# Maxima turned in mid-iteration and an expert program without a loop, in a one-core convolution, attention and expert kernel

## The chip, the core and the metric

The kernel runs on one core of a Trainium2 chip. A core has TensorE (PE, matrix products and transposes into PSUM banks), VectorE (DVE), ScalarE (ACT), GpSimd (POOL) and SyncE (SP, which here only issues DMA transfers). Each engine works through its own program in order; they meet at semaphores. The metric is the device time of the whole program in microseconds, the median of the runs.

## What is computed

The input is x, 16 images of 128 channels and 32 x 32 pixels. A convolution attention block is added to it, then, with pixels as tokens of 128 channels, a causal attention block, then a mixture of eight experts of which each token uses two. All of it is in float32.

```python
x = x + _L0_conv_ref(_gn(x), ...)      # 8 heads of queries, keys and values from a strided depthwise convolution
t = _to_tokens(x)
t = t + _L1_attn_ref(_ln_t(t), L1_attn_WQ, L1_attn_WK, L1_attn_WV)
t = t + _L1_ffn_ref(_ln_t(t), L1_ffn_router_w, L1_ffn_w1, L1_ffn_w2, L1_ffn_w3)

# in _L0_conv_ref
attn = jnp.einsum('bnqd,bdl->bnql', q, k) / HEAD_DIM ** 0.5
attn = jax.nn.softmax(attn, axis=-1)
ctx = jnp.einsum('bnql,bld->bnqd', attn, v)

# in _L1_ffn_ref: gates holds the weights of the two best experts of a token, 0 for the others
h = jax.nn.silu(h1) * h3
y = jnp.einsum('neh,ech->nec', h, w2)
out = jnp.einsum('ne,nec->nc', gates, y)
```

## The kernel before

Three stages run one after the other, each a block with its own program for each engine.

**Convolution attention** (conv_attention). Each image has 32 rows of queries; four rows are a pair's work (PAIR_ROWS), so an image is a period of PAIRS = 8 iterations. For a softmax without overflow each score needs its row's maximum. PE computes the scores of a row into one of two s_bank banks (L600), DVE reduces them to negated maxima (row_max, L395), four times per pair. PE then turns the pair's maxima into rows (turn_maxes, L608, m_bank), ACT copies the high part (max_high, L482), DVE the low part (max_low, L401), and SP puts both under the queries by two small transfers (shift_rows). PE later computes the scores again, transposed and with the maxima already subtracted (shifted_scores, L618), ACT takes exponentials (exps, L489), PE sums the values (values, L630, o_bank), ACT copies the context, PE turns it (turn_context, L638), DVE divides by the sums (normalise, L413 and L415). All this is spread over iterations: in iteration i PE scores pair i + 3 (LEAD = 3), turns the maxima of pair i + 2, computes the shifted scores of pair i, sums pair i - 1 and turns the context of pair i - 2. Iterations 0, 2, 4 and 6 also have a chunk of queries (L565), 1 the convolution (L543), 3 and 7 an output projection (L586), 7 a group mean (group_means, L526), which needs DVE's statistics (L346). The order on each engine is written out by hand in its `period`.

**Attention and routing** (attention_and_routing) is not touched. It writes every token twice, once per chosen expert, into a table in HBM sorted by expert, and a list of 2 x 136 = 272 tiles of 128 rows with the expert of each.

**Expert tiles** (expert_tiles). Each tile n passes through: SP loads its rows (L1443) into one of RING = 8 buffers, when the scatter of tile n - 8 has landed (y_sent); PE turns them (turn_rows, L1549, x_bank); ACT and DVE split them into a high and a low part (L1480, L1516); PE multiplies with w1 and w3 of the tile's expert (up, L1563 and L1566, six products of 342 columns); ACT takes silu (L1494), DVE multiplies by it and by the gate (L1531); PE turns the hidden rows (turn_hidden, L1574, three transposes), ACT copies them (L1485); PE multiplies with w2 (down, L1582, six passes), DVE copies y (L1522), POOL adds it to the output rows by an indirect transfer (L1457). PE's order for tile n is: expert number of n, rows of n + 1, up n, hidden of n - 1, down n - 2.

The helper over_tiles writes this as 34 turns of eight tiles: two turns straight, 15 in a loop, 16 in a second loop, one straight. In the loops tile numbers and semaphore values are registers. The expert number is read from the list in SBUF into a register by expert_of (L1554); down takes the number that up read, except in tiles 0 and 1 of a turn, which read it again:

```python
down(n - 2, i % 2, experts[i - 2] if i >= 2 else expert_of(n - 2))
```

## Time and profile before

| | us |
|---|---|
| median of 3 runs | 2365.29 (2364.75 to 2367.83) |
| profiled execution | 2363.08 |
| its span, first to last instruction | 2361.3 |
| convolution attention, to about | 860 |
| attention and routing, about | 880 to 1700 |
| expert tiles, first turned rows to last product | 1711 to 2352 |

The profile is one execution. "Busy" is the time in which an engine had an instruction; matmuls overlap and their ends are modelled, so a small idle time of PE is larger in truth. PEld is the loading of PE's stationary operand, PEq and PEldq are PE's sequencer, SPq is SP's queue. A bracket in the order of time gives the idle time of the engine just before an instruction and whose work ended it; "issue" means that the profile shows nothing it waited for. The granted clock is the share of 2.4 GHz that PE had.

### The profile page before, as it was taken

How to read it: one execution, taken by the hardware profiler on the slowest of the kernel's cores; microseconds unless marked ns; L12 is line 12 of the kernel's file. 1: busy time of each engine (PE TensorE's matmuls, PEld its weight loads, DVE VectorE, ACT ScalarE, POOL GpSimd, SP SyncE). 2: the span in 40 equal slices, each digit the busy share in tenths (PEclk: the TensorE clock that was granted, in tenths of full speed). 3: DMA queues.
4: the chain of work that ended last, by engine and by line, in shares of the span. 5: the costliest groups of instructions: out<-in, count | busy, mean ns of one | idle time of the engine just before them, and what ended most of it. 6: DMA issues, size and time to landing. Idle time of an engine off the chain costs nothing. (4 is left out here: it accounts for less than half of the span.)

```text
span 2361.3 us, 46450 instructions
## 1 busy us (share of the span) xinstructions
PE 2031.8 (86%) x11636; PEld 1462.9 (62%) x11637; DVE 1444.6 (61%) x4059; ACT 997.0 (42%) x2116; POOL 1006.0 (43%) x1345
## 2 busy tenths in 40 slices
PE   5999999999999974988888878886099999999998
PEld 4555555555555532655555555554098888888887
DVE  4666666666666642787677777876444444444443
ACT  1455554545555531433333333332044444444443
POOL 2121221212122111145544544555467777777776
PEclk7999999999999996999999999998599999999999
DMA  5222222222222212011111111111134444444443
GB/s 198 61 68 59 69 60 63 66 58 68 57 68 62 63 66 86 19 38 59 46 41 57 44 45 45 53 38 47 55 51 57 56 56 57 57 58 57 56 56 47
DMA packets 175904, 139.58 MB, mean 59 GB/s; under 512 B 33694, under 2 KB 163142, under 8 KB 175558
## 3 DMA queue, kind: packets, MB, share of 16 engines
q0 software_dynamic: 55808, 52.50, 13.9%
q1 hardware_dynamic: 120005, 86.09, 13.1%
q8 instruction: 31, 0.51, 0.1%
q14 instruction: 60, 0.48, 0.1%
HBM read 31.47 MB, written 46.71 MB: 33 GB/s over the span
## 5 line engine op out<-in xcount | busy, mean ns | idle before, releaser
L1457 POOL DMA_INDIRECT out<-f_y,f_rows x272 | 424.1, 1559 | 45.4 <-POOL f_waited L1455 39.8
L395 DVE TENSOR_REDUCE neg_max<-s_bank 128x2 f32<-128x512 f32 x512 | 329.9, 686 | 172.0 <-PE s_bank L600 171.5
L1531 DVE SCALAR_TENSOR_TENSOR f_hidden<-f_silu,f_rows,f_h_bank 128x341 f32<-128x341 f32 x272 | 155.2, 571 | 259.7 <-ACT f_silu L1494 206.9
L489 ACT ACTIVATE probsT<-st_bank 128x512 f32<-128x512 f32 x512 | 277.4, 593 | 36.6 <-PE st_bank L618 35.4
L975 POOL DMA_INDIRECT routed<-a_rows,a_target_idx x256 | 252.2, 985 | 74.5 <-issue 74.5
L1305 PE MATMUL a_score_bank<-a_eT,a_gT 128*128 128x512 f32 x512 | 253.2, 619 | 19.6 <-DVE a_causal_probs L1043 11.0
L630 PE MATMUL o_bank<-probsT,v_ones 128*64 128x512 f32 x1024 | 249.4, 608 | 0.0
L287 POOL TENSOR_TENSOR waited<-nothing 128x1 int32<-128x1 int32 x64 | 12.1, 190 | 547.5 <-DVE q_low L384 547.4
L1582 PE MATMUL f_y_bank<-w,f_hiddenT 114*128 (+1 forms) x1632 | 233.1, 278 | 0.9 <-DVE f_y L1522 0.6
L1494 ACT ACTIVATE f_silu<-f_h_bank 128x341 f32<-128x341 f32 x272 | 124.2, 457 | 211.1 <-PE f_h_bank L1566 164.3
L1582 PEld LDWEIGHTS f_y_bank<-w,f_hiddenT 114*128 114x128 f32 (+1 forms) x1632 | 203.2, 191 | 12.2 <-issue 11.4
L600 PEld LDWEIGHTS s_bank<-k_stack,q_stack 96*128 96x128 f32 x1024 | 141.7, 194 | 108.4 <-issue 106.4
L1563 PE MATMUL f_h_bank<-f_w_high,f_xT_high 128*128 x544 | 199.5, 369 | 0.0
L600 PE MATMUL s_bank<-k_stack,q_stack 96*128 96x256 f32 x1024 | 191.5, 310 | 6.0 <-DMA q_stack<-q_high 5.2
L962 POOL TENSOR_TENSOR a_causal_probs<-a_causal_probs,a_tril 128x128 f32<-128x128 f32 x128 | 58.2, 455 | 305.5 <-ACT a_causal_probs L1217 304.5
L1217 ACT ACTIVATE a_causal_probs<-a_score_bank,a_row_neg_max 128x128 f32<-128x128 f32 (+7 forms) x128 | 94.7, 740 | 220.1 <-DVE a_row_neg_max L1035 204.6
L618 PE MATMUL st_bank<-q_stack,k_stack 98*128 98x512 f32 x512 | 184.2, 439 | 0.1
L1563 PE MATMUL f_h_bank<-f_w_low,f_xT_high 128*128 x544 | 173.0, 320 | 0.0
L1035 DVE TENSOR_REDUCE a_row_neg_max<-a_score_bank 128x1 f32<-128x1024 f32 x128 | 156.7, 1224 | 22.7 <-PE a_score_bank L1305 22.0
L1322 PE MATMUL a_sum_bank<-a_val,a_causal_probsT 128*128 128x128 f32 x1152 | 153.9, 280 | 2.6 <-issue 2.3
L1322 PEld LDWEIGHTS a_sum_bank<-a_val,a_causal_probsT 128*128 128x128 f32 x1152 | 143.1, 195 | 10.5 <-issue 6.9
L1305 PEld LDWEIGHTS a_score_bank<-a_eT,a_gT 128*128 128x128 f32 x512 | 91.1, 198 | 90.1 <-issue 77.2
(197 smaller groups left out, 3647.6 us busy)
## 6 DMA issues: line engine op xcount, KB each, us to landing
q_stack<-q_high SPq DMA_DIRECT2D x512, 64.0 KB, 2.4
f_rows<-routed SPq DMA_DIRECT2D x272, 66.0 KB
q_stack<-q_low POOLq DMA_DIRECT2D x256, 64.0 KB, 2.6
a_staged<-X SPq DMA_DIRECT2D x16, 512.0 KB, 3.0
out<-X SPq DMA_DIRECT2D x16, 512.0 KB
X<-in_x SPq DMA_DIRECT2D x1, 6144.0 KB, 22.1
out<-f_y,f_rows POOLq DMA_INDIRECT x272
q_stack<-max_rows SPq DMA_DIRECT2D x256, 4.0 KB
```

Of the source, the lines that this page charges most:

```text
L395: dve.tensor_reduce(neg_max[:, i % 2, CT * j:CT * (j + 1)], s_bank[h % 2][:], AX_X, ALU.max, negate=True).then_inc(max_ready, 1)
L489: act.activation(probsT[:, i % 2, c, lt, :], st_bank[lt][:], ACT.Exp).then_inc(exp_done, 1)
L600: last = pe.matmul(s_bank[h % 2][:, t, :], q_stack[0:STACK, h, t * P:(t + 1) * P], k_stack[0:STACK, slot, :], start=(t == 0), stop=(t == C ...
L618: pe.matmul(st_bank[lt][:], k_stack[:, slot, lt * P:(lt + 1) * P], q_stack[:, h:h + 2, :].rearrange("p h c -> p (h c)"), start=True, stop= ...
L630: last = pe.matmul(o_bank[HALF * c:HALF * (c + 1), :], v_ones[:, slot, lt, :], probsT[:, i % 2, c, lt, :], start=(lt == 0), stop=(lt == LT ...
L975: pool.indirect_dma_start(out=routed, out_offset=bass.IndirectOffsetOnAxis(ap=target_idx[:, slot, t, k:k + 1], axis=0), in_=rows[:, slot, ...
L1035: dve.tensor_reduce(neg_max[:, i % 2:i % 2 + 1], s_bank[i % 2][:], AX_X, ALU.max, negate=True).then_inc(max_ready, 1)
L1305: last = pe.matmul(s_bank[i % 2][:, 512 * h:512 * (h + 1)], gT[:, slot, i * P:(i + 1) * P], eT[:, slot, 512 * h:512 * (h + 1)], start=True ...
L1322: last = pe.matmul(o_bank[:], probsT[:, i % 2, t, :], val[:, slot, t, :], start=(t == 0), stop=(t == i))
L1457: pool.indirect_dma_start(out=out, out_offset=bass.IndirectOffsetOnAxis(ap=rows[:, i, TOKEN:TOKEN + 1].bitcast(I32), axis=0), in_=y[:, i, ...
L1563: pe.matmul(bank[:, 0:PADDED], xT_high[:, i % 2, :], parts[part][:, of_expert], start=(part == 0), stop=False, skip_group_check=True)
L1582: last = pe.matmul(y_bank[:], hiddenT[0:m, slot, j, :], w2[0:m, bass.ds(e, 1), j, :], start=(j == 0), stop=(j == CHUNKS - 1))
```

## The change

It has three parts; nothing that is computed changes.

In the convolution attention PE turns the maxima of pair i + 2 not at the head of iteration i but between scores 1 and shifted scores 1. ACT copies them between its exponentials for the first and the second half of the pair, and DVE's max_low goes behind normalise.

In the expert tiles PE's program is written out for all 272 tiles. Tile numbers and semaphore values are constants, each expert number is read once, two tiles ahead (AHEAD = 2), and kept in a register until down. The rows are turned two tiles ahead, into two x_bank banks in turn, and split into four xT buffers. PE's order becomes: up n, expert number and rows of n + 2, down n - 2, hidden of n - 1. The waits on x_out before turning rows, on gated before up and on h_out before turning the hidden rows are gone. ACT does silu before the split of the next rows, DVE the gating before it. ACT, DVE, POOL and SP keep their loops.

The scatters add to the output rows in both kernels alike.

```diff
@@ conv_attention, DVE
                             row_max(scored[0], scored[2], 1)
+                        turned = pair(b, slot, i - 2)
+                        if has(turned[0]):
+                            normalise(*turned)
                         turning = pair(b, slot, i + LEAD - 1)
                         if has(turning[0]):
                             max_low(*turning)
-                        turned = pair(b, slot, i - 2)
-                        if has(turned[0]):
-                            normalise(*turned)
@@ conv_attention, ACT
                         turning = pair(b, slot, i + LEAD - 1)
+                        if has(b):
+                            exps(b, i, 0)
                         if has(turning[0]):
                             max_high(*turning)
                         if has(b):
-                            exps(b, i)
+                            exps(b, i, 1)
@@ conv_attention, PE
-                        if has(turning[0]):
-                            turn_maxes(*turning)
                         if has(b):
                             shifted_scores(b, slot, i, 0)
...
                         if has(scored[0]):
                             scores(*scored, 0)
                             scores(*scored, 1)
+                        if has(turning[0]):
+                            turn_maxes(*turning)
                         if has(b):
                             shifted_scores(b, slot, i, 1)
@@ expert_tiles, ACT
                     act.wait_ge(x_turned, n + 1)
-                    wait(act, h_full, n - 1)
-                    act.activation(xT_high[:, slot, :], x_bank[:], ACT.Copy).then_inc(x_high_done, 1)
+                    wait(act, h_full, n - 2 * AHEAD + 1)
+                    act.activation(xT_high[:, slot, :], x_bank[slot % 2][:], ACT.Copy).then_inc(x_high_done, 1)
...
-                    if not last_one(n):
-                        x_evacuate(n + 1, (i + 1) % 2)
                     act.wait_ge(h_full, n + 1)
                     wait(act, gated, n - 1)
                     act.activation(silu[:, i % 2, :], h1_bank[i % 2][:, 0:HIDDEN], ACT.Silu).then_inc(silu_done, 1)
+                    if not beyond(n + AHEAD):
+                        x_evacuate(n + AHEAD, (i + AHEAD) % (2 * AHEAD))
@@ expert_tiles, PE
-                def turn_rows(n, q, i):
-                    pe.wait_ge(row_in[i], 16 * (q + 1))
-                    wait(pe, x_out, n)
-                    pe.transpose(x_bank[:], rows[:, i, 0:P], ident[:]).then_inc(x_turned, 1)
...
+                def turn_rows(n):
+
+                    pe.wait_ge(row_in[n % RING], 16 * (n // RING + 1))
+                    pe.transpose(x_bank[n % 2][:], rows[:, n % RING, 0:P], ident[:]).then_inc(x_turned, 1)
...
-                def up(n, i, e):
+                    return pe.value_load(table[0:1, 1, n:n + 1], min_val=0, max_val=EXPERTS - 1)
+
+                def up(n, e):
+
                     pe.wait_ge(x_out, n + 1)
-                    wait(pe, gated, n - 1)
...
-                    wait(pe, h_out, n)
...
-                def body(n, q, i, k):
-                    if first(n):
-                        turn_rows(0, 0, 0)
-                    experts[i] = expert_of(n)
-                    if not last_one(n):
-                        turn_rows(n + 1, q + (i == RING - 1), (i + 1) % RING)
-                    up(n, i, experts[i])
-                    if not first(n):
-                        turn_hidden(n - 1, (i + 1) % 2)
-                    if not (isinstance(n, int) and n < 2):
-                        down(n - 2, i % 2, experts[i - 2] if i >= 2 else expert_of(n - 2))
-
-                over_tiles(pe, body)
...
+                for n in range(ALL):
+                    up(n, experts[n])
+                    if n + AHEAD < ALL:
+                        experts[n + AHEAD] = expert_of(n + AHEAD)
+                        turn_rows(n + AHEAD)
+                    if n >= 2:
+                        down(n - 2, experts.pop(n - 2))
+                    if n >= 1:
+                        turn_hidden(n - 1)
```

PE in the convolution attention, an iteration after a chunk of queries, before (the name behind "waits" is a semaphore, max_ready counts DVE's maxima):

```order
L608 MATMUL m_bank<-ident,neg_max 128x128 [waits m_low_done,max_ready]
L618 MATMUL st_bank<-q_stack,k_stack 128x512 [waits exp_done,m_in1]
L618 MATMUL st_bank<-q_stack,k_stack 128x512 [waits exp_done]
L638 MATMUL c_bank<-ident,ctxT 128x128 [waits ctx_done,ctxT_full]
L638 MATMUL c_bank<-ident,ctxT 128x128 x3
L600 MATMUL s_bank<-k_stack,q_stack 128x256 [waits max_ready,q_low_in3,q_in3]
L600 MATMUL s_bank<-k_stack,q_stack 128x256
L600 MATMUL s_bank<-k_stack,q_stack 128x256 [waits max_ready]
L600 MATMUL s_bank<-k_stack,q_stack 128x256
L618 MATMUL st_bank<-q_stack,k_stack 128x512 [waits exp_done] x2
```

and now:

```order
L620 MATMUL st_bank<-q_stack,k_stack 128x512 [waits exp_done,m_in1]
L620 MATMUL st_bank<-q_stack,k_stack 128x512 [waits exp_done]
L640 MATMUL c_bank<-ident,ctxT 128x128 [waits ctx_done,ctxT_full]
L640 MATMUL c_bank<-ident,ctxT 128x128 x3
L602 MATMUL s_bank<-k_stack,q_stack 128x256 [waits max_ready,q_low_in3,q_in3]
L602 MATMUL s_bank<-k_stack,q_stack 128x256
L602 MATMUL s_bank<-k_stack,q_stack 128x256 [waits max_ready]
L602 MATMUL s_bank<-k_stack,q_stack 128x256
L610 MATMUL m_bank<-ident,neg_max 128x128 [waits m_low_done,max_ready]
L620 MATMUL st_bank<-q_stack,k_stack 128x512 [waits exp_done] x2
```

The turn into m_bank stood first and now stands behind the four s_bank matmuls, so that the first wait on max_ready is that of s_bank.

DVE in the same iteration, before:

```order
L395 TENSOR_REDUCE neg_max<-s_bank 128x2 [waits m_full,s_full]
L395 TENSOR_REDUCE neg_max<-s_bank 128x2 [waits s_full]
L401 TENSOR_TENSOR max_rows<-m_bank,max_rows 8x128 [waits m_high_done]
L413 RECIPROCAL rsum<-c_bank 128x2x4 [waits c_full]
L415 TENSOR_TENSOR context<-c_bank,rsum 128x256 [waits rsum_ready]
L395 TENSOR_REDUCE neg_max<-s_bank 128x2 [waits s_full] x2
```

and now:

```order
L395 TENSOR_REDUCE neg_max<-s_bank 128x2 [waits m_full,s_full]
L395 TENSOR_REDUCE neg_max<-s_bank 128x2 [waits s_full]
L413 RECIPROCAL rsum<-c_bank 128x2x4 [waits c_full]
L415 TENSOR_TENSOR context<-c_bank,rsum 128x256 [waits rsum_ready]
L401 TENSOR_TENSOR max_rows<-m_bank,max_rows 8x128 [waits m_high_done]
L395 TENSOR_REDUCE neg_max<-s_bank 128x2 [waits s_full] x2
```

max_rows (max_low) went behind the two operations of normalise.

PE in the expert tiles, from the expert load before down in tile 0 of a looped turn to that of tile 1, before (TENSOR_LOAD with the two ISA behind it is one expert load; ISA and REGISTER_ALU run in PE's sequencer):

```order
L1554 TENSOR_LOAD table
L1554 ISA x2
L43 REGISTER_ALU [waits f_h_out]
L1582 ISA [waits f_y_out]
L1582 MATMUL f_y_bank<-w,f_hiddenT 128x128
L1582 ISA
L1582 MATMUL f_y_bank<-w,f_hiddenT 128x128
L1582 ISA
L1582 MATMUL f_y_bank<-w,f_hiddenT 128x128
L1554 ISA
L1554 TENSOR_LOAD table
L1554 ISA x2
```

and now, from the expert load of a tile to the head of the next up:

```order
L1557 TENSOR_LOAD table
L1557 ISA x2
L1554 MATMUL f_x_bank<-ident,f_rows 128x128 [waits f_row_in5]
L1585 ISA [waits f_y_out,f_h_out]
L1585 MATMUL f_y_bank<-w,f_hiddenT 128x128
L1585 ISA
L1585 MATMUL f_y_bank<-w,f_hiddenT 128x128
L1585 ISA
L1585 MATMUL f_y_bank<-w,f_hiddenT 128x128
L1576 MATMUL f_hT_bank<-ident,f_hidden 114x128 [waits f_gated]
L1576 MATMUL f_hT_bank<-ident,f_hidden 114x128 x2
L1566 ISA [waits f_x_out]
```

One load is left where two stood around down, the rows of a later tile are turned ahead of down, and the register operations that carried waits (REGISTER_ALU) are gone.

## Rows read from the trace of the kernel before

**Rows 1.** Busy time by stretch (PE, PEld, DVE, ACT, POOL), clock, DMA share, GB/s

```profile
37.00:860.00 823.00, 775.88 (x3852) 466.26 (x3853) 544.48 (x1158) 414.82 (x823) 150.03 (x325) 0.99 0.25 62
1713.00:2346.00 633.00, 616.65 (x4322) 565.67 (x4322) 301.31 (x811) 302.88 (x813) 467.41 (x536) 1.00 0.43 56
```

**Rows 2.** Waits in total, whole run: us, times, longest

```profile
PE m_bank L608 <- DVE neg_max L395: 40.4, 81, 1.1
```

**Rows 3.** Order of time, PE, first stage: start, us, operation, idle before

```profile
434.10 1.88 PE L586 MATMUL front<-context,owT 128*128 128x512 f32 x4
435.82 0.27 PE L608 MATMUL m_bank<-ident,neg_max 128*128 128x128 f32 x1
...
445.74 0.74 PE L600 MATMUL s_bank<-k_stack,q_stack 96*128 96x256 f32 x4
447.63 0.33 PE L608 MATMUL m_bank<-ident,neg_max 128*128 128x128 f32 x1 [1.15 <-DVE neg_max L395]
447.81 0.73 PE L618 MATMUL st_bank<-q_stack,k_stack 98*128 98x512 f32 x2
...
448.73 0.72 PE L600 MATMUL s_bank<-k_stack,q_stack 96*128 96x256 f32 x4
...
453.65 0.33 PE L608 MATMUL m_bank<-ident,neg_max 128*128 128x128 f32 x1 [0.28 <-DVE neg_max L395]
```

**Rows 4.** Order of time, PE, expert tiles in the loop

```profile
2001.78 0.27 PE L1549 MATMUL f_x_bank<-ident,f_rows 128*128 128x128 f32 x1
...
2010.61 0.33 PE L1549 MATMUL f_x_bank<-ident,f_rows 128*128 128x128 f32 x1 [0.15 <-issue]
...
2013.42 0.33 PE L1549 MATMUL f_x_bank<-ident,f_rows 128*128 128x128 f32 x1 [0.22 <-issue]
...
2020.59 0.27 PE L1549 MATMUL f_x_bank<-ident,f_rows 128*128 128x128 f32 x1
```

**Rows 5.** One line's instructions, whole run: duration min/median/max ns

```profile
L1554 PEldq TENSOR_LOAD <-table x340: 295/301/489, 1711.3 to 2349.1; - x170
```

**Rows 6.** Order of time, PE, expert tiles of the first turn

```profile
1725.53 0.27 PE L1549 MATMUL f_x_bank<-ident,f_rows 128*128 128x128 f32 x1
...
1727.60 0.28 PE L1549 MATMUL f_x_bank<-ident,f_rows 128*128 128x128 f32 x1
```

**Rows 7.** Order of time, DVE, first stage

```profile
446.28 1.29 DVE L395 TENSOR_REDUCE neg_max<-s_bank 128x2 f32<-128x512 f32 x2 [0.92 <-PE s_bank L600]
...
456.00 0.21 DVE L346 BATCH_NORM_AGGREGATE mv<-bn_st 128x2 f32<-128x12 f32 x1
```

**Rows 8.** Chain of work, 2013 to 2045 us: start, us, what

```profile
2018.81 0.63 PE f_h_bank L1563 x4
2019.44 0.32 PE f_h_bank L1566 x2
```

**Rows 9.** Groups of instructions by line, 1720 to 2340 us: mean ns, idle before

```profile
L1485 ACT ACTIVATE f_hiddenT<-f_hT_bank 114x384 f32<-114x384 f32 x265 | 128.6, 485 | 0.0
```

**Rows 10.** Order of time, POOL, at the end

```profile
2346.68 1.56 POOL L1457 DMA_INDIRECT out<-f_y,f_rows  x1 [0.15 <-POOL f_waited L1455]
...
2348.63 1.56 POOL L1457 DMA_INDIRECT out<-f_y,f_rows  x1 [0.16 <-POOL f_waited L1455]
```

**Rows 11.** Order of time, DVE and SP, two trips of the ring

```profile
2000.02 0.29 DVE L1522 COPY f_y<-f_y_bank 128x128 f32<-128x128 f32 x1
...
2004.17 0.29 DVE L1522 COPY f_y<-f_y_bank 128x128 f32<-128x128 f32 x1
...
2004.30 0.34 SPq L1443 DMA_DIRECT2D f_rows<-routed  x1
...
2008.76 0.33 SPq L1443 DMA_DIRECT2D f_rows<-routed  x1
```

**Rows 12.** The page, DMA queues (packets, MB, share), issues (KB each, us to landing)

```profile
q8 instruction: 31, 0.51, 0.1%
...
q_stack<-q_high SPq DMA_DIRECT2D x512, 64.0 KB, 2.4
```

More of the change, by code:

```diff
@@ L482, in max_high, with exps @@
                     act.activation(max_rows[:, i % 2, 0, :], m_bank[0:MAXES, :], ACT.Copy).then_inc(m_high_done, 1)
-                def exps(b, i):
-                    wait(act, o_full, pair_no(b, i) - 1)
-                    for c in range(CHUNKS_PER_PAIR):
-                        for lt in range(LT):
-                            act.wait_ge(st_full, PAIR_EXPS * pair_no(b, i) + LT * c + lt + 1)
-                            act.activation(probsT[:, i % 2, c, lt, :], st_bank[lt][:], ACT.Exp).then_inc(exp_done, 1)
+                def exps(b, i, c):
+                    if c == 0:
+                        wait(act, o_full, pair_no(b, i) - 1)
+                    for lt in range(LT):
+                        act.wait_ge(st_full, PAIR_EXPS * pair_no(b, i) + LT * c + lt + 1)
+                        act.activation(probsT[:, i % 2, c, lt, :], st_bank[lt][:], ACT.Exp).then_inc(exp_done, 1)
                 def evacuate_context(b, slot, i):
@@ L1348 @@
 PADDED = HIDDEN + 1
+AHEAD = 2
 def expert_tiles(nc, table, routed, out, ntok, ident, w1, w3, w2, weights_in):
@@ L1377, in expert_tiles @@
         y = sb("y", [P, RING, P])
-        x_bank = ps("x_bank", [P, P])
+        x_bank = [ps(f"x_bank{i}", [P, P]) for i in range(2)]
         h1_bank = [ps(f"h1_bank{i}", [P, 512]) for i in range(2)]
@@ L1423, in first, with beyond @@
             return isinstance(n, int) and n == 0
-        def last_one(n):
-            return isinstance(n, int) and n == ALL - 1
+        def beyond(n):
+            return isinstance(n, int) and n >= ALL
         def entry(n):
@@ L1488, in body @@
                     if first(n):
-                        x_evacuate(0, 0)
-                    if not last_one(n):
-                        x_evacuate(n + 1, (i + 1) % 2)
+                        for early in range(AHEAD):
+                            x_evacuate(early, early)
                     act.wait_ge(h_full, n + 1)
@@ L1525, in body @@
                     if first(n):
-                        x_low(0, 0)
-                    if not last_one(n):
-                        x_low(n + 1, (i + 1) % 2)
+                        for early in range(AHEAD):
+                            x_low(early, early)
                     dve.wait_ge(silu_done, n + 1)
@@ L1533, in body @@
                                              op0=ALU.mult, op1=ALU.mult).then_inc(gated, 1)
+                    if not beyond(n + AHEAD):
+                        x_low(n + AHEAD, (i + AHEAD) % (2 * AHEAD))
                     if not (isinstance(n, int) and n < 2):
@@ L1561, in up @@
                     for bank, parts in outs:
                         for part in range(2):
-                            pe.matmul(bank[:, 0:PADDED], xT_high[:, i % 2, :], parts[part][:, of_expert],
+                            pe.matmul(bank[:, 0:PADDED], xT_high[:, n % (2 * AHEAD), :], parts[part][:, of_expert],
                                       start=(part == 0), stop=False, skip_group_check=True)
                     for bank, parts in outs:
-                        last = pe.matmul(bank[:, 0:PADDED], xT_low[:, i % 2, :], parts[0][:, of_expert],
+                        last = pe.matmul(bank[:, 0:PADDED], xT_low[:, n % (2 * AHEAD), :], parts[0][:, of_expert],
@@ L1567, in up, with turn_hidden @@
                                          start=False, stop=True, skip_group_check=True)
                     last.then_inc(h_full, 1)
-                def turn_hidden(n, slot):
+                def turn_hidden(n):
                     pe.wait_ge(gated, n + 1)
-                    wait(pe, h_out, n)
                     for j in range(CHUNKS):
-                        last = pe.transpose(hT_bank[:, j, :], hidden[:, slot, j * CHUNK:(j + 1) * CHUNK], ident[:])
+                        last = pe.transpose(hT_bank[:, j, :], hidden[:, n % 2, j * CHUNK:(j + 1) * CHUNK], ident[:])
@@ L1575, in turn_hidden, with down @@
                     last.then_inc(h_turned, 1)
-                def down(n, slot, e):
+                def down(n, e):
                     pe.wait_ge(h_out, n + 1)
@@ L1581, in down @@
                         m = min(CHUNK, HIDDEN - j * CHUNK)
-                        last = pe.matmul(y_bank[:], hiddenT[0:m, slot, j, :], w2[0:m, bass.ds(e, 1), j, :],
+                        last = pe.matmul(y_bank[:], hiddenT[0:m, n % 2, j, :], w2[0:m, bass.ds(e, 1), j, :],
                                          start=(j == 0), stop=(j == CHUNKS - 1))
                     last.then_inc(y_full, 1)
-                def body(n, q, i, k):
-                    if first(n):
-                        turn_rows(0, 0, 0)
-                    experts[i] = expert_of(n)
-                    if not last_one(n):
-                        turn_rows(n + 1, q + (i == RING - 1), (i + 1) % RING)
-                    up(n, i, experts[i])
-                    if not first(n):
-                        turn_hidden(n - 1, (i + 1) % 2)
-                    if not (isinstance(n, int) and n < 2):
-                        down(n - 2, i % 2, experts[i - 2] if i >= 2 else expert_of(n - 2))
-                over_tiles(pe, body)
-                turn_hidden(ALL - 1, 1)
-                down(ALL - 2, 0, expert_of(ALL - 2))
-                down(ALL - 1, 1, expert_of(ALL - 1))
+                experts = {n: expert_of(n) for n in range(AHEAD)}
+                for n in range(AHEAD):
+                    turn_rows(n)
+                for n in range(ALL):
[7 more added lines that the diff above has]
+                        turn_hidden(n - 1)
+                down(ALL - 2, experts.pop(ALL - 2))
+                turn_hidden(ALL - 1)
+                down(ALL - 1, experts.pop(ALL - 1))
 def build(nc, dram, out):
```

10 lines of the change are left out of this document (4 added, 6 removed).

## The prediction

> **What bounds the kernel now.** I read the page first, for where PE is busy, then the busy time of each stretch, then each stage's order of time on TensorE (PE). The program has three stages that do not overlap: the convolution attention (37 to 860 us), attention with routing (880 to 1700 us) and the expert tiles (1711 to 2352 us). In the first and the third PE is busy 94% and 97% of the time, at a granted clock of 0.99 and 1.00, its upper level of 2.4 GHz [rows 1]; VectorE (DVE), ScalarE (ACT) and GpSimd (POOL) all stand well below that. The change touches these two stages alone. Attention with routing, 820 us, keeps its program, and I cost it at nothing.
>
> In the first stage the order of time shows where PE is not fed. An iteration is one pair: shifted scores 0, turned context, scores 0 and 1, shifted scores 1, values, scores 2 and 3, and sometimes queries or a projection. It begins with the turn of the maxima (m_bank, L608), and that turn waits for the fourth row maximum of the pair scored just before: 40.4 us in 81 waits [rows 2]. After queries the idle time shown is 0.28 us, after a projection none, and in the one iteration of eight that has neither 1.15 us [rows 3]. A shown idle time begins at the modelled end of the matmul before, and where nothing waits the next one starts 0.16 us before that end (434.10 + 1.88 against 435.82). So a wait really costs 0.16 us more than is shown: 40.4 + 81 x 0.16 = **53 us**.
>
> In the third stage the wait table holds nearly nothing for PE, yet tiles differ. From one x_bank transpose to the next, tiles of the loop take from 2.05 to 2.81 us (2010.61 to 2013.42 is one of two that take 2.81); eight take 18.81 [rows 4]. The slow ones begin with an idle time that ends on "issue": no engine was late, PE's own sequencer was. Tiles 0 and 1 of a turn load two expert numbers where the others load one: 340 loads for 272 tiles [rows 5]. The first turn of eight is written without a loop in this kernel already, and there a tile takes 2.07 us [rows 6], its neighbours 2.05 and 2.06. That is the pace of PE itself on this work.
>
> **Part 1, the maxima turned later.** The m_bank turn goes behind scores 1. What is late next is scores 0, which needs the third row maximum of the pair before (its bank), and scores 1, which needs the fourth. In the iteration without extra work scores 3 end near 446.32 and the fourth maximum at 446.28 + 1.29 = 447.57 [rows 3, 7]. Shifted scores 0 and the context take 447.81 to 448.73 = 0.92 us, scores 0 0.24 more, so scores 1 would come at 447.48, 0.1 to 0.15 us too early. Once in each of 16 images: 2.4 us stay. After queries their matmuls come on top and nothing stays.
>
> A second wait takes back a part. In iteration 7 the group mean (L526) waits for DVE's statistics, which end at 456.00 + 0.21 whenever PE comes; PE now comes 0.44 us earlier (0.28 + 0.16) and waits it out [rows 3, 7]. With 14 such iterations: 6 us back. ACT's copy of the maxima now stands between the exponentials of shifted scores 0 and 1. It lasts 0.27 us; ACT is busy 415 of 823 us [rows 1] and idle 0.3 us just there, before the second pair of exponentials, so I take nothing, and 0.1 us in each of 128 iterations, 13 us, as the bad bound. DVE copies the low part after normalising, 0.6 us later, and SP's two small transfers follow it; their result is needed only two iterations, some 12 us, later. On SP they keep their place behind the queries' transfers. Nothing is queued that could not wait. Sum of stage one: 53 - 2 - 6 = **45 us**, between 28 and 53.
>
> **Part 2, TensorE's expert program.** It removes 68 expert loads, the register arithmetic for tile numbers and wait values, the loop, and the waits on buffers that other waits imply. Each tile is left with one load. The price of the doubled load is in the rows: a slow tile 2.81 against 2.06. If every tile ran at 2.06, a turn would take 16.5 instead of 18.8. The Trainium skill ("DMA: Bandwidth & Descriptors", Latency and other measured facts) gives a tensor load a floor of about 600 ns; the row's instruction is 0.30 us long, and the whole slow tile 0.75 longer. By the page alone the 68 loads would be an estimated 41 us.
>
> Two blocking waits stay in PE's stream: x_out before up, h_out with y_out before down. With the new order (up, turn of rows n+2, down n-2, turn of hidden n-1) I time them: up is 0.63 + 0.32 = 0.95 us [rows 8], x 0.11, down 0.67 and hidden 0.33, sum 2.06. From the start of hidden's turn to h_out: 0.49 for the three transposes, 0.05 to ACT, 0.48 for ACT's copy [rows 9] = 1.02, and 0.16 until PE can use it (the gap from DVE's maximum to PE's matmul is 0.06, 447.57 to 447.63 [rows 3, 7]; the rest is the sequencer's own step). The following up and x hide 0.33 + 0.95 + 0.11 = 1.39. Slack 0.2 us. For y: DVE does hidden, x_low and then y in a row after silu, and y ends 2.63 us into a tile, again 0.3 before the next down. POOL needs 1.95 us for a scatter back to back [rows 10], just under 2.06. So no engine but PE bounds the tile.
>
> **The ring of eight row buffers** is nearer. A row load for tile n+8 goes out only when the scatter of tile n has landed. From DVE's y copy to that load pass 4.28 us (2000.02 to 2004.30) and 4.59 us (2004.17 to 2008.76) [rows 11]; the load's landing is not shown, the nearest row is a 64 KB transfer on the same queue, 2.4 us [rows 12]. Trip: 6.7 to 7.0 us. Now rows are turned one tile earlier (two tiles ahead, though at the end of up), and y is copied as late as 2.34 us into its tile: with a tile of T us the ring has 3T + 0.95 - 0.29 = 3T + 0.66, that is 6.84 at T = 2.06. The trips need T = 2.01 to 2.11. PE takes tiles in order, so the later trips set the pace: I take **2.11 us**, 16.9 us a turn. 31 turns stand in the loops: 31 x (18.8 - 16.9) = 59; the turns at both ends bring 1 more. Stage three: **60 us**, between 37 (T = 2.20) and 77 (T = 2.05: 31 x 2.4 + 3).
>
> The tail after the last matmul is POOL's scatters and stays. The profiled execution took 2363.1 us, 2361.3 of it span; 2363.1 - 45 - 60 = 2258. The median of the runs lies 2.2 us above the profiled one, so **2260 us**.
>
> **The rivals.**
> Forecast, around 2260 (2240 to 2278): 0.52.
> *The ring binds harder*: scatters and loads come closer together and a trip takes 7.3 us or more; T = 2.20 or above, stage three gives 37 or less, the time is 2283 to 2300. For it: two trips read close together already differ by 0.3 us, and one part in ten more is enough. Against it: the DMA engines are busy 43% of the time only [rows 1]. The fast first turn says nothing here, since its rows were loaded ahead. 0.20. The Trainium skill ("DMA: Bandwidth & Descriptors", Queues, rings and completion order) says that a DMA engine goes round its queues packet by packet; the straight program adds code packets to those engines, which no run here shows next to the ring. It is counted in this rival.
> *The first stage's wait only moves*: to scores 0 or to the exponentials, leaving 10 us of 45; 2295. Against it: PE has 0.92 us of other work ahead of scores 0. 0.10.
> *Neither binds*: T = 2.05 and all 53 us: 2235. 0.10.
> *Slower*: code. A straight program has to be fetched; a loop is not. The run had 31 packets, 0.51 MB, of code on queue 8 [rows 12]. If PE's sequencer sat out a fetch as long as a 64 KB load, 2.4 us, every four tiles, that is 68 x 2.4 = 163 us against the 105 gained: 2423. It decides from 3.1 us a turn (105 over 34). Against it: the straight first turn ran at PE's own pace [rows 6]. 0.04. The Trainium skill ("Runtime: NRT & Kernel Launch", Instruction fetch mechanics) calls such crossings mostly hidden; the straight turn agrees.
> *It does nothing*: the slow tiles are slow for another reason than the second load, and the maxima's gain is lost: within 0.2%. 0.02. Between the cases lie the other 0.02.
>
> **How the numbers follow.** The range runs from the floor of 2235 to 2300, where the ring at T = 2.20 meets a small loss in stage one. It holds the forecast's case (0.52), about 0.14 of the ring's, 0.08 of the moved wait's and 0.09 of the floor's, 0.83 in all. A measurement of this kernel can tell about 0.2%, 5 us, from no change. Only the last two rivals are not clearly faster, and a little is left for a mixture of losses: faster 0.94, same 0.02, slower 0.04.
>
> **What would show it.** In stage one the m_bank wait vanishes from PE's table, a wait of some 0.1 us on scores 1 appears once an image, and L526 waits about 0.4 us longer. The stage ends near 815 us instead of 860. In stage three eight tiles take 16.4 to 17 us, all alike; 272 loads. If x_bank waits for a DMA, the ring has become the bound and T tells by how much; if PE idles on "issue", the sequencer still is; if on DVE or ACT, my slacks of 0.2 and 0.3 us were wrong. I would be wrong altogether if tiles without a loop ran no faster than 2.3 us.

## The result and the profile after

| | before | after |
|---|---|---|
| median, us | 2365.02 (2363.98 to 2367.83) | 2262.70 (2261.8 to 2264.08) |
| ratio, 95% interval | 1 | 0.9566 (0.955 to 0.9583) |
| profiled execution, its span | 2363.08, 2361.3 | 2261.92, 2260.1 |
| first to last turn of the maxima | 815.2 | 770.8 |
| first turned rows to last product of down | 639.7 | 582.9 |
| behind the last product | 10.3 | 10.0 |

The kernel became 102.3 us faster; 2260 had been forecast, 105 less. Busy time by stretch of the kernel after (the columns are those of [rows 1]):

```profile
37.00:818.00 781.00, 767.33 (x3868) 476.24 (x3870) 539.77 (x1161) 402.91 (x828) 155.12 (x325) 0.99 0.26 65
1668.00:2241.00 573.00, 564.20 (x4294) 550.23 (x4295) 262.71 (x807) 302.40 (x808) 464.83 (x533) 1.00 0.47 63
```

PE is now busy 98% of both stretches (before 94 and 97%) at the same granted clock. The two durations of the table come from the first and last start of three lines. First the kernel before, then after (duration min/median/max in ns, first and last start in us):

```profile
L608 PE MATMUL m_bank<-ident,neg_max x128: 269/328/476, 36.7 to 851.9; 128*128 128x128 f32 x128
L1549 PE MATMUL f_x_bank<-ident,f_rows x272: 274/275/449, 1711.3 to 2343.7; 128*128 128x128 f32 x136
L1582 PE MATMUL f_y_bank<-w,f_hiddenT x1632: 273/275/373, 1718.6 to 2351.0; 114*128 x182
```

```profile
L610 PE MATMUL m_bank<-ident,neg_max x128: 272/273/415, 38.0 to 808.8; 128*128 128x128 f32 x128
L1554 PE MATMUL f_x_bank<-ident,f_rows x272: 270/272/467, 1667.2 to 2241.5; 128*128 128x128 f32 x136
L1585 PE MATMUL f_y_bank<-w,f_hiddenT x1632: 272/275/373, 1674.2 to 2250.1; 114*128 x182
L1557 PEldq TENSOR_LOAD <-table x272: 295/301/490, 1665.6 to 2239.9; - x136
```

815.2 - 770.8 = 44.4 us went out of the first stage, 639.7 - 582.9 = 56.8 out of the third. The loads are 272, one for each tile.

**First stage.** All that PE waits for between 37 and 818 us (us in total, times, longest):

```profile
PE front L528 <- DVE mv L346: 12.6, 15, 2.3
PE st_bank L620 <- DMA q_stack<-max_rows: 0.5, 1, 0.5
PE m_bank L610 <- DVE neg_max L395: 0.2, 1, 0.2
PE s_bank L602 <- DVE neg_max L395: 0.2, 1, 0.2
```

Of the 40.4 us of [rows 2], 0.2 are left. The group mean (L528) waits 12.6 us; before it waited 7.0:

```profile
PE front L526 <- DVE mv L346: 7.0, 15, 1.9
```

The small stall at scores 1 is in no wait table, since the modelled ends of the matmuls cover it; it stands in the order of time, in the iteration that has no extra work:

```profile
425.97 0.99 PE L602 MATMUL s_bank<-k_stack,q_stack 96*128 96x256 f32 x4
426.80 0.27 PE L610 MATMUL m_bank<-ident,neg_max 128*128 128x128 f32 x1
...
431.60 0.72 PE L602 MATMUL s_bank<-k_stack,q_stack 96*128 96x256 f32 x4
432.16 0.28 PE L610 MATMUL m_bank<-ident,neg_max 128*128 128x128 f32 x1
...
433.82 0.38 PE L528 MATMUL front<-mv,group_mean 128*128 128x1 f32 x2 [0.73 <-DVE mv L346]
```

From scores 0 to the turn it is 0.83 us (425.97 to 426.80), in the next iteration 0.56: scores 1 wait 0.27 us, once an image. In this iteration DVE works through the maxima without a gap:

```profile
425.11 2.67 DVE L395 TENSOR_REDUCE neg_max<-s_bank 128x2 f32<-128x512 f32 x4 [1.16 <-PE s_bank L602]
```

**Third stage.** PE's wait table for 1668 to 2252 us, whole:

```profile
PE f_x_bank L1554 <- DMA f_rows<-routed: 6.8, 11, 1.4
PE f_y_bank L1585 <- ACT f_hiddenT L1488: 1.3, 2, 0.7
PE f_x_bank L1554 <- issue: 1.1, 1, 1.1
PE f_h_bank L1566 <- DVE f_xT_low L1520: 0.6, 1, 0.6
```

From one row turn to the next a tile takes 2.056 us in the median and (2241.5 - 1667.2) / 271 = 2.119 in the mean. What lifts the mean are single tiles. In the order of time:

```profile
2204.71 0.27 PE L1554 MATMUL f_x_bank<-ident,f_rows 128*128 128x128 f32 x1
2207.81 0.33 PE L1554 MATMUL f_x_bank<-ident,f_rows 128*128 128x128 f32 x1 [0.88 <-DMA f_rows<-routed]
2210.05 0.27 PE L1554 MATMUL f_x_bank<-ident,f_rows 128*128 128x128 f32 x1
```

Rows came late (3.10 us for the tile), and the tile behind it took 2.24 instead of 2.056. Such late turns, most of them shorter and many under the threshold of the wait table, make up the rest: 66 of the 271 turn-to-turn times are over 2.1 us.

The page has more code than [rows 12], 1.13 MB for 0.51, and no wait of PE goes with it. The DMA queues by stretch show where it is fetched: 7 packets of code in the whole stage before (1713 to 2346 us), 45 after (1668 to 2241 us), and one of them within the late tile above (2204.71 to 2207.81 us). The page first, then the three stretches:

```profile
q8 instruction: 69, 1.13, 0.2%
q8 instruction: 7, 0.11, 0.1%
q8 instruction: 45, 0.74, 0.5%
q8 instruction: 1, 0.02, 1.9%
```

The packets come every 12.6 us, once in six tiles, and the late turns keep their company. From 1712 us on, 117 of 248 turns start within 6 us of the start of a packet. Of the 60 that came over 2.1 us after the turn before, 52 are among these 117, and so are 15.3 of the 16.7 us that the tiles take above 2.056. In the five executions of this expert program together it is 62.0 of 79.5 us, in under half of the tiles. So the code does not hold up PE, but most of the long trips of the rows fall together with its packets. No run changed the packets alone; that they lengthen the trips is an inference from this timing.

### The profile page after: what moved, and what is told of

Same layout as the page of the kernel before. It is cut to its first block and busy times, and to the rows that moved or that the text cites. A ratio compares the mean times of both kernels' runs of the same rounds, so it can differ in the third digit from the quotient of the medians.

```text
span 2260.1 us, 45057 instructions
## 1 busy us (share of the span) xinstructions
PE 1970.1 (87%) x11636; PEld 1459.5 (65%) x11636; DVE 1401.3 (62%) x4059; ACT 983.6 (44%) x2116; POOL 1011.6 (45%) x1345
## 3 DMA queue, kind: packets, MB, share of 16 engines
q8 instruction: 69, 1.13, 0.2%
## 5 line engine op out<-in xcount | busy, mean ns | idle before, releaser
L620 PE MATMUL st_bank<-q_stack,k_stack 98*128 98x512 f32 x512 | 213.5, 484 | 0.6 <-DMA q_stack<-max_rows 0.5
L602 PE MATMUL s_bank<-k_stack,q_stack 96*128 96x256 f32 x1024 | 196.2, 312 | 6.7 <-DMA q_stack<-q_high 6.0
L1488 ACT ACTIVATE f_hiddenT<-f_hT_bank 114x384 f32<-114x384 f32 x272 | 133.7, 492 | 144.4 <-issue 82.9
```

What stands on the lines that cost most here:

```text
L602: last = pe.matmul(s_bank[h % 2][:, t, :], q_stack[0:STACK, h, t * P:(t + 1) * P], k_stack[0:STACK, slot, :], start=(t == 0), stop=(t == C ...
L620: pe.matmul(st_bank[lt][:], k_stack[:, slot, lt * P:(lt + 1) * P], q_stack[:, h:h + 2, :].rearrange("p h c -> p (h c)"), start=True, stop= ...
```

## The experiments

The stages of all kernels are compared by their traces, first to last start as above (us): turns of the maxima, and rows to last product. The ratio is that of the whole time to the kernel before on the same chip.

| kernel | maxima | expert tiles | ratio (95%) |
|---|---|---|---|
| before | 815.2 | 639.7 | 1 |
| after | 770.8 | 582.9 | 0.9566 (0.9550 to 0.9583) |
| only_maxima | 771.2 | 639.5 | 0.9774 (0.9747 to 0.9802) |
| only_experts | 815.5 | 578.1 | 0.9756 (0.9729 to 0.9784) |
| one_load | 815.2 | 591.7 | 0.9783 (0.9756 to 0.9810) |
| ring12 | 771.2 | 563.7 | 0.9470 (0.9443 to 0.9498) |
| stats_early | 756.8 | 580.1 | 0.9494 (0.9463 to 0.9525) |
| rows_first | 771.2 | 662.2 | 0.9895 (0.9870 to 0.9921) |
| twice_loaded | 771.4 | 599.8 | 0.9645 (0.9614 to 0.9676) |
| both12 | 756.8 | 563.9 | 0.9426 (0.9406 to 0.9446) |
| copied_twice | 770.5 | 579.7 | 0.9566 (0.9539 to 0.9592) |
| turn_only | 921.6 | 582.3 | 1.0197 (1.0170 to 1.0224) |
| no_loads | 770.7 | 587.6 | 0.9553 (0.9523 to 0.9583) |
| rows_first_no_loads | 770.5 | 649.7 | 0.9799 (0.9746 to 0.9852) |

The first stage repeats within 1 us. The third repeats within 5: five executions of one and the same expert program (after, only_experts, stats_early, copied_twice, turn_only) took 582.9, 578.1, 580.1, 579.7 and 582.3. Attention and routing between them (last projection to first row turn), which no kernel here changes, took from 802 to 840 us (839.9 in the kernel after, 813.3 in ring12). That is why whole times are not read to a few us here, and stages are.

### Each part alone

only_maxima is the first hunk of the change (all of conv_attention) without the others, only_experts the rest without the first.

> The kernel before with the changes in the convolution attention alone. My terms: the m_bank wait of 53 us goes, 2.4 us come back at scores 1 (0.16 once in each of 16 images) and 5.6 at the group mean (its wait 7.0 before, 12.6 after): 2365 - 45 = 2320 us, and the expert tiles as before, 639.8 us from the first turned rows to the last product. Rival: the two parts of the change are not independent (the second stage or the code fetch reacts), then the time is more than 5 us away from 2320.

> The kernel before with the changed expert tiles alone. The third stage took 582.9 us after against 639.8 before, 57 less: 2365 - 57 = 2308 us. The two parts alone then sum to 102, the whole change measured 102.3. Rival: they overlap or help each other, and the sum is off by more than 5 us.

The changed stage's line of only_maxima, then of only_experts:

```profile
L610 PE MATMUL m_bank<-ident,neg_max x128: 272/273/416, 37.5 to 808.7; 128*128 128x128 f32 x128
```

```profile
L1552 PE MATMUL f_x_bank<-ident,f_rows x272: 270/272/469, 1680.4 to 2250.1; 128*128 128x128 f32 x136
```

Each stage behaves as in the whole change and as if the other were not there: 44.0 us and 61.6. The whole times fell by 50.8 and 57.1 us on a chip on which the kernel before took 2332.9; the sum is 108, where 102 was expected. That is over the 5 us named as the sign of parts that depend on each other, and so is the first by itself (50.8 for 45). But the intervals of the ratios run from 46 to 59 us and from 50 to 63, so the whole times cannot decide it, and by the stages the excess of the first is not in its stage.

### What a second expert load costs

```diff
-                        down(n - 2, i % 2, experts[i - 2] if i >= 2 else expert_of(n - 2))
+                        down(n - 2, i % 2, experts[max(i - 2, 0)])
```

> The kernel before, with its loops, waits and register arithmetic, but tiles 0 and 1 of a turn take an expert number that is in a register already (of another tile, so their last product uses another expert's weights): the second load is left out, nothing else. If the doubled load was the whole price of the slow tiles, eight tiles fall from 18.8 to about 16.7 us (the looped tile's other six take 2.05 to 2.1), 31 x 2.1 = 65 us: 2300 us, no slower than the written-out program of the change in this stage. If the loop and its register arithmetic carried half of it, 2330. If the loads cost only their 0.30 us each, 62 x 0.30 = 19: 2346.

The stage fell by 48.0 us to 591.7. PE has 274 expert loads here for 340 before, 66 less (not 68: tiles 0 and 1 of the first turn have no down), so a load cost 0.73 us. That is most of what the whole expert program brings, and less than the 65 expected. The loop is left with two slow tiles at its head (order of time of one_load):

```profile
2002.16 0.27 PE L1549 MATMUL f_x_bank<-ident,f_rows 128*128 128x128 f32 x1
2004.66 0.32 PE L1549 MATMUL f_x_bank<-ident,f_rows 128*128 128x128 f32 x1 [0.18 <-issue]
2006.92 0.27 PE L1549 MATMUL f_x_bank<-ident,f_rows 128*128 128x128 f32 x1
2008.98 0.27 PE L1549 MATMUL f_x_bank<-ident,f_rows 128*128 128x128 f32 x1
```

2.50 and 2.26 us, then 2.06. PE still sits idle on "issue" at the head of a turn, with one load for each tile. Over the whole stage the medians of the eight tiles are 2.47, 2.27, 2.06, 2.05, 2.05, 2.19, 2.07 and 2.07: five of eight tiles run at PE's own pace with the old order of PE, its single x_bank and its extra waits, so most of what is left comes with the head of the loop's turn. Whether it is the branch or the register arithmetic was not separated, and why the sixth tile takes 2.19 neither. Together it is 28 us (591.7 to ring12's 563.7, below); the written-out program removes them too, but hands back 14 to 19 us to late rows.

The opposite test puts the second load back into the written-out program:

```diff
-                        down(n - 2, experts.pop(n - 2))
+                        e = experts.pop(n - 2)
+                        down(n - 2, expert_of(n - 2) if n % 8 < 2 else e)
```

> The changed kernel, still without a loop, with the expert number read a second time before down in tiles 0 and 1 of every eight, as before the change (68 loads more). If the load itself is what a slow tile cost, the 0.75 us come back in most of them: 68 x 0.6 to 0.75 = 41 to 51 us, a stage of 624 to 634. If the loop made the second load dear and PE's sequencer otherwise runs far enough ahead to hide it, the stage stays at 583.

599.8 us: 17 more than after, 0.26 for each of 66 loads (338 for 272). Neither case came true. In the order of time of twice_loaded:

```profile
2002.05 0.27 PE L1554 MATMUL f_x_bank<-ident,f_rows 128*128 128x128 f32 x1
2004.32 0.27 PE L1554 MATMUL f_x_bank<-ident,f_rows 128*128 128x128 f32 x1
2006.66 0.27 PE L1554 MATMUL f_x_bank<-ident,f_rows 128*128 128x128 f32 x1
```

And in its waits:

```profile
PE f_y_bank L1585 <- issue: 7.0, 22, 0.6
```

2.27 and 2.34 instead of 2.056. This turn is one of the better ones: over the stage the two tiles have a median of 2.41, and together they take 0.72 us a turn more than in the kernel after, while the other six take 0.22 less, with 8 waits for rows in the table instead of 11. So a load costs 0.36 us in its tile, and 0.26 in the stage. The same load costs 0.73 us in the loop: it has no price of its own. I read it as what PE's sequencer then needs above PE's own 2.056 us, a sequencer that in the loop needs the whole tile, with its register arithmetic, and without has some 0.37 us (0.73 - 0.36) to spare. Its total was not measured by itself.

The Trainium skill ("DMA: Bandwidth & Descriptors", Latency and other measured facts) has a tensor load at about 600 ns at least. Here the two differ: the instruction is 0.30 us long in the row of L1557 above, and what it took from a tile was 0.36 us in one program and 0.73 in the other.

### What holds the tile above 2.056

ring12 is the kernel after with twelve row and y buffers; the turns are of twelve tiles, the middle and the last one partly straight.

```diff
-RING = 8
+RING = 12
```

> The changed kernel with twelve row and y buffers instead of eight. A row load then has four tiles, 8 us, more before its rows are turned. If late rows are what lifts the mean tile from its median of 2.056 to 2.119 us, the wait of x_bank on the row load vanishes, every tile takes 2.05 to 2.06, the mid-way drain of the scatters is hidden too, and the stage loses 271 x 0.063 = 17 us: 2246 us. If only the waits shown for x_bank (6.8 us) go, and the tile of 2.24 us behind each of them has a cause of its own, 2256. If the ring isn't it, 2263.

```profile
L1555 PE MATMUL f_x_bank<-ident,f_rows x272: 270/272/472, 1640.7 to 2196.0; 128*128 128x128 f32 x136
L1586 PE MATMUL f_y_bank<-w,f_hiddenT x1632: 272/275/372, 1647.8 to 2204.4; 114*128 x182
```

563.7 us, 19 less than after and 14 to 19 less than its five executions; (2196.0 - 1640.7) / 271 = 2.049 in the mean. In its waits for the stage no DMA is named any more:

```profile
PE f_x_bank L1555 <- issue: 41.4, 1, 41.4
PE f_y_bank L1586 <- ACT f_hiddenT L1489: 1.3, 2, 0.7
PE f_h_bank L1567 <- DVE f_xT_low L1521: 0.6, 1, 0.6
```

(The 41.4 us stand before the first tile.) The ring was the whole difference between median and mean. The code packets are as many as in the kernel after, 45, and behind the first tiles none takes over 2.1 us: with four buffers more a long trip costs nothing. The 6.8 us that PE shows as waiting for rows were less than half of its price.

rows_first makes the ring tighter instead: the rows of n + 2 are turned ahead of up n.

```diff
                 for n in range(ALL):
-                    up(n, experts[n])
                     if n + AHEAD < ALL:
-                        experts[n + AHEAD] = expert_of(n + AHEAD)
+                        pe.wait_ge(x_out, n + 1)
                         turn_rows(n + AHEAD)
+                    up(n, experts[n])
+                    if n + AHEAD < ALL:
+                        experts[n + AHEAD] = expert_of(n + AHEAD)
```

> The changed kernel with the rows of tile n + 2 turned ahead of up of tile n, not behind it: the ring loses 0.95 us, so that a trip has 3T - 0.29 instead of 3T + 0.66. From DVE's y copy to the landed rows a trip takes 6.43 us in the median (6.73 at the upper quartile) in the changed kernel. If the ring holds the tile, T = (6.43 to 6.73 + 0.29 + 0.04) / 3 = 2.25 to 2.35 in the mean instead of 2.12, every tile waits for its rows, and the stage takes 612 to 639 us instead of 583. If PE's own work is the bound and the ring only a coincidence, nothing changes.

```profile
PE f_x_bank L1554 <- DMA f_rows<-routed: 28.9, 43, 2.2
PE f_x_bank L1554 <- DVE f_xT_low L1520: 2.4, 7, 0.5
```

The waits for rows went from 11 to 43, the stage to 662.2 us: 0.95 us taken from the ring cost 79, more than the 29 to 56 expected. The ring decides, as the first case said, but its size was wrong, and by the wait table not every tile waits for its rows. The edit also puts the expert load behind the wait for the rows; the median tile takes 2.33 us, and 2.08 without the loads (rows_first_no_loads). The two kernels without expert loads were meant to say why.

```diff
-                        experts[n + AHEAD] = expert_of(n + AHEAD)
+                        experts[n + AHEAD] = experts[n]
```

> The changed kernel without the expert loads of tiles 2 to 271: each tile takes the expert that is in a register since the start (so most products use another expert's weights, the work is the same). In the changed kernel a tile behind a wait for rows takes 2.24 us instead of 2.055. If that is the expert load, which PE's sequencer no longer does ahead after a wait, those tiles fall to 2.06; the waits for rows stay, and the stage takes about 576 to 580 us. If the 2.24 has another cause, they stay at 2.24.

> The kernel with the rows turned ahead of up, without its expert loads as above. There the stage took 662 us, 79 more than the changed kernel, where I had expected 29 to 56 from the ring. In its trace 43 us stand ahead of the row turns and 28 us at the first product of down, behind the expert load. If the load behind the wait is what came on top, the stage falls by about 28 us to 634 and the mean tile to 2.31 us, the ring's own price. If the ring alone is the price, the time freed at down reappears ahead of the row turns and the stage stays near 662.

In no_loads the tile behind a wait takes 2.11 us (1954.86 to 1956.97; 2.11 to 2.13 in all 18 cases) instead of 2.24:

```profile
1951.46 0.27 PE L1554 MATMUL f_x_bank<-ident,f_rows 128*128 128x128 f32 x1
1954.86 0.33 PE L1554 MATMUL f_x_bank<-ident,f_rows 128*128 128x128 f32 x1 [1.18 <-DMA f_rows<-routed]
1956.97 0.27 PE L1554 MATMUL f_x_bank<-ident,f_rows 128*128 128x128 f32 x1
```

So 0.13 of the 0.18 us behind a wait are the expert load: while PE's stream stands at row_in, its sequencer gets ahead with nothing. The other 0.05 us were not looked into. But the stage did not shrink. It took 587.6 us, outside the expected 576 to 580 and above all five executions with the loads, and the waits for rows grew to 18.4 us from 6.8:

```profile
PE f_x_bank L1554 <- DMA f_rows<-routed: 18.4, 18, 1.6
```

This trace is of the slowest of four executions, though, 2264.2 us for a median of 2253.5, and copied_twice, with all loads, has a median of 2253.4 on the same chip. That the stage gained nothing is as much as can be said; a gain of the expected 3 to 7 us is inside the spread.

rows_first_no_loads took 649.7 us: 12.5 of the expected 28 came off, and its waits for rows rose from 28.9 to 58.9 us. By the whole times it is more, 0.9895 to 0.9799 or about 23 us, with intervals that allow 4 to 41. So where the ring holds the pace, work taken from PE turns in part into waiting; how large the part is stays open. Why some trips are long was not settled: of the trips in the kernel after, the upper tenth took over 7.1 us and the longest 8.5 against a median of 6.4, in scatters as well as in loads. Most of the lost time falls together with packets of code (above), not all of it, and no experiment changed the transfers or the packets themselves.

### ACT's part in the first stage

```diff
+                    act.activation(spare[:, i % 2, :], m_bank[0:MAXES, :], ACT.Copy)
                     act.activation(max_rows[:, i % 2, 0, :], m_bank[0:MAXES, :], ACT.Copy).then_inc(m_high_done, 1)
```

> The changed kernel with ACT copying the high part of the maxima twice, the first time into a buffer that nobody reads: one operation of 0.27 us more between the exponentials of each of 128 iterations. I took ACT's copy there at nothing, because ACT is idle around it: then the first stage stays as it is (turns of the maxima 771 us apart, first to last, within 2 us). If ACT's chain is what paces the iterations with queries, where it works without a gap, 64 x 0.27 = 17 us come on top; if it always does, 35 us.

770.5 us: nothing, with 0.27 us more in each iteration. ACT has room.

```diff
-                        if has(b):
-                            exps(b, i, 0)
                         if has(turning[0]):
                             max_high(*turning)
                         if has(b):
+                            exps(b, i, 0)
                             exps(b, i, 1)
```

> The changed kernel with ACT's copy of the maxima ahead of both exponentials, as before the change; PE's turn stays in mid-iteration. Shifted scores 1 need a bank that the exponentials of shifted scores 0 free, and those now stand behind the copy, which waits for the turn. From the turn: 0.28 us for it, about 0.1 to ACT, 0.27 the copy, 0.6 the first exponential, so PE waits some 1.2 us in each of 128 iterations: 150 us more in the first stage (921 us from the first turn to the last instead of 771). If ACT's order does not matter, 771.

921.6 us, as expected. PE's waits in the first stage of turn_only:

```profile
PE st_bank L619 <- ACT probsT L489: 109.3, 126, 1.0
```

0.87 us shown in each iteration, 1.18 in truth (150.8 / 128). That is net: the group mean's wait fell from 12.6 to 1.9 us. The 0.16 us that the prediction adds to a shown wait would make 1.03 of 0.87, so that rule does not carry over to this wait. PE's move without ACT's new order makes the whole kernel 2% slower than before. The edit that cost nothing was the one that made the other possible.

### The group mean, and both together

```diff
-                        if i == PAIRS - 2 and has(b + 2):
+                        if i == PAIRS - 3 and has(b + 2):
                             channel_stats(b + 2)
```

> The changed kernel with DVE's channel statistics of the image after next one iteration earlier (after the maxima of iteration 5 instead of 6). If the group mean's wait in iteration 7 is all that is left to gain there, it goes: 14 times 0.73 us shown + 0.16 = 12.5 us less in the first stage (turns of the maxima 770.8 us apart first to last, then 758). If DVE's 1.5 us of statistics only hold up the row maxima of iteration 6 instead, a wait on scores appears and the gain is 5 us or less.

> Twelve buffers and the earlier statistics together. The ring alone took the third stage from 582.9 to 563.7 us; the statistics should give 12.5 in the first: the ratio to the kernel before should be about 0.947 - 0.005 = 0.942. If both draw on the same time (the DMA queues, or DVE), it stays at 0.947.

A line of stats_early and the largest wait left in its first stage:

```profile
L610 PE MATMUL m_bank<-ident,neg_max x128: 272/273/416, 38.3 to 795.1; 128*128 128x128 f32 x128
```

```profile
PE s_bank L602 <- DVE neg_max L395: 1.8, 4, 1.0
```

The wait of L528 is gone, 14.0 us with it (770.8 to 756.8; 12.5 expected). With the ring of twelve the gains add up: 756.8 and 563.9 us, a ratio of 0.9426 (0.9406 to 0.9446) to the kernel before. That is faster than both kernels of this case, about 1.5% below the one after.

## Why the prediction held, step by step

**The wait on m_bank, 53 us.** Right: it vanished. The stage measured 44.4 us less where 45 were forecast (53 - 2.4 - 6).

**Scores 0 and 1.** Right in the place, too small in size: once an image scores 1 come late, by 0.27 us where 0.1 to 0.15 had been worked out, so 16 x 0.27 = 4.3 us came back instead of 2.4. The sum then is 53 - 4.3 - 5.6 = 43, and 44.4 were measured.

**The group mean gives back 6 us.** Right: 12.6 - 7.0 = 5.6. That it was a wait of its own is shown by stats_early.

**ACT's copy at nothing.** Right, by copied_twice, and the bad bound of 13 us was too careful. The text costed the copy alone; that its place between the exponentials is worth 151 us was not in it. DVE's move of max_low behind normalise was not tested by itself.

**The doubled load.** The total came out, the reason only in part. The prediction put a slow tile's 0.75 us on the second load and let everything fall to 2.06 once it was gone. In the loop a load costs 0.73, but removing it there leaves 2.50 and 2.26 at the head of each turn. The loads are worth 48 us and the loop with its register arithmetic 28; 14 to 19 of these come back as late rows, which leaves the 57 to 62 of the stage. In the written-out program the same load costs 0.36 in its tile. The prediction also counts 68 loads where 66 went. What the rest of this part is worth (PE's new order, the second x_bank, the dropped waits, the order on ACT and DVE) no run shows by itself.

**The slacks of 0.2 and 0.3 us.** Right. ACT's and DVE's rows of the kernel after, and PE's down:

```profile
1997.87 0.49 ACT L1488 ACTIVATE f_hiddenT<-f_hT_bank 114x384 f32<-114x384 f32 x1 [0.49 <-issue]
1997.93 0.28 DVE L1526 COPY f_y<-f_y_bank 128x128 f32<-128x128 f32 x1
1998.72 0.83 PE L1585 MATMUL f_y_bank<-w,f_hiddenT 114*128 x6
```

h_out is done at 1998.36 and y_out at 1998.21, 0.36 and 0.51 us before down; less the 0.16 that PE needs, 0.2 and 0.35.

**The ring, T = 2.11.** The mean was 2.119, the cause the one named, and the picture wrong. "All alike" had been forecast; in fact three tiles of four run at 2.056, and a late trip costs a tile up to 1.6 us, plus 0.18 in the next. The trip was put at 6.7 to 7.0 us from two cases; its median is 6.4, and its upper tail does the damage. That the two come to the same mean is partly luck: rows_first, by the same sum, came out 23 us above the upper end.

**The rivals.** "Neither binds" is what ring12 is: T = 2.05, so the floor of the prediction was real and the ring kept the kernel from it. "The ring binds harder" is rows_first, with 0.95 us less to spare. "Code" as the prediction drew it, a sequencer that sits out its fetches, did not show: 1.13 MB and not one wait on "issue" but the 1.1 us above. The Trainium skill ("Runtime: NRT & Kernel Launch", Instruction fetch mechanics) calls the crossing from one block of code to the next mostly hidden; for PE the trace agrees. The other road is one the prediction only mentioned under the ring, code packets on the DMA engines that also carry the rows, and it is the one for which the traces speak: most of the time above 2.056 us a tile falls within 6 us of a packet, and the ring of eight has no margin for it.

Attention and routing and the tail stayed, 839.9 for 837.8 us and 10.0 for 10.3.

## What to carry to other kernels

When slow iterations idle on "issue", sum up everything that the engine's sequencer does in one; here the same load cost 0.73 us in one program and 0.36 in another, so do not multiply the length of one instruction by its count. A ring of buffers needs a margin for its late trips, not for the median: here four more buffers, 8 us of margin, were worth 14 to 19 us that the wait table showed as 7. When a loop is written out, look at the DMA queues by stretch: its code travels there too. Before moving an operation of the bounding engine, look at what its consumer has queued behind it: the same move brought 44 us with ACT's order changed and lost 106 without.

## What the runs showed of the hardware

A blocking wait on PE costs more than its own length. In the kernel after, the tile behind each of the 13 that took over 2.4 us took 2.23 to 2.25 us instead of 2.056. Without the expert load it took 2.11 to 2.13 in 18 cases, so 0.13 us of it are work that the sequencer otherwise does ahead.

With the loop written out, packets of code of 16 KB came every 12.6 us (45 in the stage for 7), one of them took about 0.9 us of a DMA engine's time (1.9% of 16 engines in 3.1 us), and no wait of PE goes with them. The five executions with a ring of eight lost 62.0 of their 79.5 us within 6 us of a packet; the one with a ring of twelve and the same 45 packets lost nothing.

A stage that no kernel changed took from 802 to 840 us, and it went with the chip: 801.6 to 813.3 us in eight traces from one, 831.8 to 837.8 in four from another, 837.8 and 839.9 in those of before and after. The kernel before took 2365.0, 2332.9, 2327.8 and 2354.9 us in the four comparisons, 1.6% apart, more than several of the effects measured here. It is not the clock or the work: in only_maxima, 30 us shorter there than before, the granted clock is 0.91 in both and PE is busy 612 us for 610. What makes the engines wait less on one chip was not looked into.
